# Sixteen Gram matrices per image: one f32 product of W with itself in place of three f16 products of its halves

## The reference

```
def _L0_conv_ref(W, num_iters):
    n = W.shape[-1]
    absW = jnp.abs(W)
    norm1 = jnp.max(jnp.sum(absW, axis=-2), axis=-1)
    norminf = jnp.max(jnp.sum(absW, axis=-1), axis=-1)
    scale = (norm1 * norminf)[..., None, None]
    X = jnp.swapaxes(W, -1, -2) / scale
    two_I = 2.0 * jnp.eye(n, dtype=W.dtype)
    for _ in range(num_iters):
        X = jnp.matmul(X, two_I - jnp.matmul(W, X))
    return X
...
x = x + _L0_conv_ref(_gn(x), 5)
```

## Time and profile before

| what | value |
|---|---|
| median of the runs | 4549.56 us (3 runs, 4548.0 to 4550.94) |
| the profiled execution | 4556.31 us |
| its span | 4554.5 us |
| PE busy | 4378.0 us, 96% of the span |
| DVE busy | 3841.3 us, 84% |
| ACT busy | 2249.5 us, 49% |
| POOL busy | 2606.1 us, 57% |
| part A | to about 2470 us |
| part B | the rest |

### The profile page before, as it was taken

One profiled execution on the slowest core, in us unless ns is written; L12 is line 12 of the kernel. 1 busy time (PEld: TensorE's weight loads), 2 busy tenths in 40 slices (PEclk: granted clock), 3 DMA queues, 4 the chain that ended last, 5 costly groups with the idle time before them and its releaser, 6 DMA issues. The chain is left out here.

```text
span 4554.5 us, 69799 instructions
## 1 busy us (share of the span) xinstructions
PE 4378.0 (96%) x24265; PEld 3031.8 (67%) x24265; DVE 3841.3 (84%) x8224; ACT 2249.5 (49%) x4551; POOL 2606.1 (57%) x2957
## 2 busy tenths in 40 slices
PE   6999999999999999999997799999999999999998
PEld 6888888888888888888886344444444444444443
DVE  7999999999999999999995777777877877877774
ACT  4777777777777777777775222222222222222221
POOL 7888888888888888888885222222222222222221
PEclk9999999999999999999998899999999999999999
DMA  1111111111111111111111455555555555555553
GB/s 56 58 56 58 55 60 54 55 56 56 56 56 56 56 57 56 56 57 57 57 56 44 103 134 134 133 131 131 138 129 133 137 128 133 138 129 131 138 132 84
DMA packets 333608, 403.52 MB, mean 89 GB/s; under 512 B 23088, under 2 KB 286032, under 8 KB 316880
## 3 DMA queue, kind: packets, MB, share of 16 engines
q1 hardware_dynamic: 308688, 334.25, 29.5%
q10 hardware_dynamic: 24576, 64.79, 5.5%
HBM read 135.22 MB, written 134.22 MB: 59 GB/s over the span
## 5 line engine op out<-in xcount | busy, mean ns | idle before, releaser
L286 POOL TENSOR_TENSOR M<-two,YX 128x256 f32<-128x256 f32 x2560 | 1823.0, 738 | 341.6 <-ACT YX L361 317.1
L756 PE MATMUL bank<-YX,M 128*128 128x256 f32 x8192 | 1930.5, 384 | 0.0
L1163 PE MATMUL bank<-xn,wt 128*128 128x512 f16 (+1 forms) x6912 | 1660.7, 381 | 25.1 <-DVE xn L1019 17.5
L756 PEld LDWEIGHTS bank<-YX,M 128*128 128x128 f32 x8192 | 1494.5, 190 | 179.7
L361 ACT ACTIVATE YX<-bank 128x512 f32<-128x512 f32 x2048 | 1226.7, 599 | 632.2 <-PE bank L756 626.2
L937 POOL TENSOR_TENSOR xn<-F,xn 128x2048 f16<-128x2048 f32 x128 | 487.5, 3809 | 1574.1 <-ACT xn L973 1574.1
L1163 PEld LDWEIGHTS bank<-xn,wt 128*128 128x128 f16 (+1 forms) x6912 | 672.9, 100 | 810.8 <-issue 20.1
L1037 DVE SCALAR_TENSOR_TENSOR x<-bank,wu,x 128x512 f32<-128x512 f32 x512 | 382.3, 747 | 338.7 <-PE bank L1170 329.8
L1170 PE MATMUL bank<-xh,wth 96*128 96x512 f16 (+1 forms) x1792 | 516.2, 381 | 11.2 <-DMA xh<-xn 11.2
L973 ACT ACTIVATE xn<-F 128x2048 f16<-128x2048 f32 x128 | 244.8, 1912 | 566.5 <-DVE F L1093 566.5
L978 ACT ACTIVATE sd<-ve 128x1 f32<-128x1 f32 x128 | 25.9, 203 | 716.5 <-DVE ve L1074 391.4
(11 more groups left out here) (107 smaller groups left out, 3582.9 us busy)
## 6 DMA issues: line engine op xcount, KB each, us to landing
X<-in_x SPq DMA_DIRECT2D x64, 1024.0 KB, 4.8
x_scratch<-X SPq DMA_DIRECT2D x64, 1024.0 KB, 5.4
x<-x_scratch SPq DMA_DIRECT2D x64, 1024.0 KB, 8.3
out<-x SPq DMA_DIRECT2D x64, 1024.0 KB, 3.8
xh<-xn SPq DMA_DIRECT2D x384, 131.8 KB, 4.5
xh<-xn ACTq DMA_DIRECT2D x384, 131.8 KB, 5.4
xh<-xn SPq DMA_DIRECT2D x192, 65.9 KB, 2.4
xh<-xn ACTq DMA_DIRECT2D x192, 65.9 KB, 2.4
```

The costliest lines, as they stand in the source:

```text
L286: nc.gpsimd.tensor_tensor(M[odd][:, at, :], two[:, :].unsqueeze(1).broadcast_to([H, 2, H]), YX[odd][:, at, 0:H], ALU.subtract).then_inc(ma ...
L756: ins = nc.tensor.matmul(banks[u % A_RING][:, 2 * H * m:2 * H * (m + 1)], M[odd][:, 2 * p + m, :], YX[odd][:, 2 * p + m, :], start=True, s ...
L1163: nc.tensor.matmul(bank, wt[l][:, a, k, :], v, start=(k == a == b == 0), stop=False)
```

## The change

W is kept in two buffers, chosen by the image's number, and W16 goes away with `upper_w` and `lower_w`. `grams` multiplies the f32 tile W with itself, once for each matrix. It now waits for `w_done`, which DVE gave one step earlier. `normalise`, which writes the other buffer, now waits for the transposes and Gram matrices of the image before the last in place of the last one's.

```
-            W = sb("W", [H, C, H])
-            W16 = sb("W16", [H, 2, C, H], f16)
+            W = [sb(f"W{n}", [H, C, H]) for n in range(2)]
...
-                                if prep and k == 0 and p % 2 == 1:
-                                    lower_w(i + 1, p // 2)
...
-                    for q in range(QUADS):
-                        lower_w(0, q)
...
-                            if prep and u < 8 and u % 2 == 1:
-                                upper_w(i + 1, u // 2)
...
-                    for q in range(QUADS):
-                        upper_w(0, q)
...
-                            need(dve, t_ps, 4 * n)
-                            need(dve, w_lower, QUADS * n)
-                        ins = nc.vector.tensor_scalar(group_of(W, g), group_of(X[slot], g), m0[:, g:g + 1],
+                            need(dve, t_ps, 4 * n - 4)
+                            need(dve, g_ps, 4 * n - 4)
+                        ins = nc.vector.tensor_scalar(group_of(W[n % 2], g), group_of(X[slot], g), m0[:, g:g + 1],
                                                       r0[:, g:g + 1], ALU.subtract, ALU.mult)
...
                         for q in range(q0, q1):
-                            pe.wait_ge(w_lower, QUADS * n + q + 1)
+                            pe.wait_ge(w_done, n + 1)
...
                             for m in range(4):
-                                for a, b in ((0, 0), (0, 1), (1, 0)):
-                                    ins = nc.tensor.matmul(banks[4 + q % 2][:, m * H:(m + 1) * H],
-                                                           W16[:, a, 4 * q + m, :], W16[:, b, 4 * q + m, :],
-                                                           start=(a, b) == (0, 0), stop=(a, b) == (1, 0))
+                                ins = nc.tensor.matmul(banks[4 + q % 2][:, m * H:(m + 1) * H],
+                                                       W[n % 2][:, 4 * q + m, :], W[n % 2][:, 4 * q + m, :],
+                                                       start=True, stop=True)
```

More of the change, by code:

```diff
@@ L184, in conv_net @@
             w_done = sem("w_done")
-            w_upper = sem("w_upper")
-            w_lower = sem("w_lower")
             t_ps = sem("t_ps")
@@ L274, in _ @@
                             nc.gpsimd.memset(xn[l][n][:, :, :], 0.0).then_inc(pads_zeroed, 1)
[L276 to L281, removed]
                     def factor(odd, p, made):
@@ L322, in sqrt @@
                         nc.scalar.activation(sd[k][:, :], ve[k][:, :], ACT.Sqrt).then_inc(sqrt_done[k], 1)
[L324 to L330, removed]
                     def distance(n, slot, g):
@@ L501, in row_sums @@
                         need(dve, norm_t, n)
-                        nc.vector.tensor_reduce(absum[:, 0:C], W[:, :, :], AX.X, ALU.add,
+                        nc.vector.tensor_reduce(absum[:, 0:C], W[n % 2][:, :, :], AX.X, ALU.add,
                                                 apply_absolute_value=True).then_inc(rows_summed, 1)
@@ L712, in transposes @@
                                 ins = nc.tensor.transpose(banks[4 + q % 2][:, m * H:(m + 1) * H],
-                                                          W[:, 4 * q + m, :], idt[:, :])
+                                                          W[n % 2][:, 4 * q + m, :], idt[:, :])
                             ins.then_inc(t_ps, 1)
```

## The result

The changed kernel takes 4565.05 us (median of 7 runs, 4563.36 to 4567.09), the kernel before 4548.0 us in the same session (7 runs, 4546.45 to 4551.33). The ratio is 1.0034, interval 1.0024 to 1.0044: slower, by 17 us between the medians. The profiled execution takes 4566.47 us against 4556.31 before: 10.2 us more, where the sum of the prediction gave 10.8.

What follows compares the result with a forecast made beforehand. Part A was taken as bound by PE's stream of matmuls. The terms +46.8 + 1.8 - 30.2 - 7.6 = +10.8 on the profiled 4556.31 gave 4567.1 us; allowing for profiling's possible cost, 4563 us was forecast, range 4552 to 4583.

Steps and rivals of the forecast that it cites:

- PE's own work: Gram matrices on PE, f32 in place of f16 products: 0.74 us a step more, +46.8 us over 63 images.
- The broadcast: PE's weight load at `norm_broadcast`: with `lower_w` off POOL the wait for `ndiag` goes, 0.33 us idle stays; -30.2 us.
- Quad 3: PE's 0.12 us wait for POOL's last M ahead of quad 3 of `last_products` goes in 63 steps: -7.6 us.
- The first image: Preparation ahead of the first step: 16 f32 records take 3.6 us in place of 2.7, in two halves; +1.8 us.
- The sum: All terms together against the profiled execution's 4556.31 us: +10.8, giving 4567.1 us; forecast median 4563 us.
- `ndiag` late: Rival at the broadcast, 12%: small DVE instructions pass once per factor, `ndiag` 0.65 us late each step; 40 us more, 4603 us.
- The 0.33 us going too: Rival "no slower", 14%: the idle time left at the broadcast goes with the wait; 20 us less, 4543 us, or half, 4553.
- One record for an f32 product: Rival "faster", 3%: each Gram matrix on PE is issued as one record, like the transposes; 4443 us.
- A new starvation in the run of 17 factors: Rival, 5%: a DVE instruction is held to the end of POOL's run, `final` some 4 us late a step; up to 4800 us.

Runs made afterwards that it cites:

- The kernel without `lower_w`: Kernel before with W16's lower half zeroed once and never rewritten, so Gram matrices lack two cross terms: 4522.3 us against 4566.9, ratio 0.9901.
- the kernel with the split kept: Changed kernel with `upper_w` and `lower_w` back on ACT and POOL, W16 unread, Gram products still f32: 4595.1 us against 4566.9 for the kernel before, ratio 1.0065.
- the one with `lower_w` spread: Kernel before with `lower_w` moved to after pairs 1 and 5 of round 0 and pairs 0 and 4 of round 2: 4583.7 us against 4566.9, ratio 1.0035.

## Why the prediction was right

**PE's own work.** 0.74 us a step was forecast. Measured: from the start of a quad to the start of the next run it is 0.98 us for quad 0 and 0.89 for the others, 3.65 in all, where four times 0.73 stood before: 0.73 more. By the length of the steps it is 38.07 - 37.54 + 0.12 + 0.12 = 0.77, with the two waits taken off. Taking `last_products` as the nearest row gave the pitch to 0.001 us.

**The broadcast.** The long and the short waits are both gone, and 0.33 us stay, in each step. All idle time there was 51.2 us (50.7 for `ndiag`, 0.5 at two other places) and is 21.1, so 30.1 less, where 30.2 were forecast. The kernel without `lower_w` shows that POOL's relief does this alone; the kernel with the split kept shows that without it nothing of it comes. The prediction let L426 take up to one factor. It comes 0.20 us before the end of a factor and gets through in the gap of 0.14 us behind it, in 0.23 us. What `ndiag` waits for now is PE itself: `norms` stands idle for 0.58 us until the turned sums come.

**Quad 3.** Gone as forecast, 3.91 to 3.74 us, of which 0.05 is the first gap.

**The first image.** +1.8 us forecast. From the first to the second `row_sums` it is 25.76 us, 24.05 before: 1.7 more. The third begins 1.4 us later, but the step between them differs by up to 2.9 us from one execution to the next for the same kernel, so this says nothing more.

**The sum.** +10.8 against +10.2 in the profiled executions. The median moved by 17.05 us, and this was the one open point: the prediction gave two readings of the 6.75 us by which the profiled execution of before stood above its median, a cost of profiling or more long waits, and took the middle, 4563. It is no cost of profiling: the changed kernel's profiled executions are 1.4 us above their median in one session and 1.7 below it in the other. More long waits are the likely reading, since the kernel before was seen with 10, 24 and 30 of them, but they were not counted in the runs that made the median, and the start can move too. If nothing else moved them, the medians in the three sessions differ by some 20 long waits, at 0.96 us each.

That the time came out right wasn't luck. The same sum made from the two later profiles of the kernel before, with their waits of 56.3 and 36.9 us, gives 4558.5 + 5.2 = 4563.7 and 4539.3 + 24.6 = 4563.9 us, and from the first one 4567.1; the changed kernel was measured at 4563.2 to 4567.1. That +10.8 met +10.2 to 0.6 us was in part luck, since the start alone moves an execution by up to 4 us. And the size of the change, +17 in one session and +10.6 in another, belongs to the session of the kernel before.

**The rivals.** `ndiag` late: fell, it comes a microsecond early. The 0.33 us going too: fell, they stand in all steps. One record for an f32 product: fell. A new starvation in the run of 17 factors: not seen in the changed kernel.

So even whether the change counts as slower hangs on the kernel before. In the session at 4566.9 us it was no faster than the changed kernel's 4565, which wasn't timed there.

Left open is what decides between 0.66 and 3.4 us. The same instruction meets the same factor, the second behind the last `lower_w`, at the same distance (0.07 to 0.11 us behind its start) in both kinds of step, and nothing here shows why the share of long ones goes from 10 to 30 of 62 for one and the same kernel.

## What to carry to other kernels

Price a change of number format by the pitch of records of the same type and width that the trace already has, and count the gap behind the run too. Ask next what the removed helper work did to the engine beside it: here the 298 us of POOL were worth 30 us of PE through one small instruction of DVE. The same gain was to be had for nothing by moving that work to where POOL has gaps and DVE's chain isn't short, in rounds 0 and 1; with half of it in round 2 the kernel was 17 us slower. And the time of a kernel with such a race should be read together with the count in its profile, and not from one median.

## What the runs showed of the hardware that was not expected

- A small DVE instruction that comes while POOL works through factors, one every 0.69 us without a pause, can be held over the factor in progress and the four behind it, 3.3 to 3.4 us, to the end of the run, and in the next step for 0.66 us only. It happened to a tensor_scalar of 8 columns and to a tensor_tensor of 16, always to the first one. In the long steps those behind it came after the end of the run; in the short ones each, the first too, took about one factor.
- The same happened beside four memsets of 4.0 us: 6.55 us for a tensor_scalar of 8 columns in some executions, 2.48 us in others.
- Where the factor was followed by a gap (0.11 to 0.14 us in four kernels, 1.1 us in the one with `lower_w` spread), the instruction ended 0.03 us behind it, and the long hold never came.
- A weight load of 32 rows between loads of 128 stood idle for 0.33 us although its operand was there a microsecond earlier, in every step of the changed kernel.
- Behind products of 16 columns an f32 run is longer by 0.08 to 0.09 us (1.97 against 1.89 us for 256 columns, 1.14 against 1.05 for a Gram quad); an f16 quad at that place is 0.83 us, as elsewhere.
